# Self attention of the first layer: from pairs of tiles, phase by phase, to four tiles staggered in one step

## What is computed

```
xn = layernorm(x)                                   # over 256 values
q, k, v = xn @ in_proj.T + in_proj_bias             # 16 heads of 16
s = q @ k.T / 4 + alibi_slope[head] * (j - i)       # row i, column j, causal
p = maximum(softmax(s), 1e-10)
x = x + (p @ v) @ out_w.T + out_b
```

## Time and profile before

| | us |
|---|---|
| median of three runs | 8161.44 |
| the profiled execution: its time | 8200.94 |
| the profiled execution: its span | 8199.2 |
| TensorE matmul busy in the span | 6635.7 (81%) |
| VectorE busy | 5436.6 (66%) |
| ScalarE busy | 4031.7 (49%) |
| GpSimd busy | 2661.4 (32%) |

### The profile page before, as it was taken

How to read it: one execution, slowest core, us unless ns; L and a number is a source line. 1 busy time by engine, 2 the same in 40 slices (tenths; PEclk the granted TensorE clock), 3 DMA queues, 4 the chain that set the end, 5 groups by cost and what they waited for, 6 DMA issues and landing times. The chain is left out here.

```text
span 8199.2 us, 201722 instructions
## 1 busy us (share of the span) xinstructions
PE 6635.7 (81%) x71072; PEld 4742.2 (58%) x71073; DVE 5436.6 (66%) x11534; ACT 4031.7 (49%) x7817; POOL 2661.4 (32%) x4595
## 2 busy tenths in 40 slices
PE   5666999987727888888888888888888888799484
PEld 4556899964414555555555555555555555588442
DVE  5556666654237777777777777777778877544464
ACT  1112333321216666666666666666666666355121
POOL 0000000012124455454554554554555555200402
PEclk7777888888958888888988898988889988688597
DMA  0000000011210000000000000000000000000212
GB/s 28 0 0 15 5 4 4 4 43 55 88 42 12 14 11 13 13 11 13 13 11 13 11 13 13 13 11 13 11 13 13 13 11 14 8 10 8 95 61 92
DMA packets 136074, 172.62 MB, mean 21 GB/s; under 512 B 29104, under 2 KB 110096, under 8 KB 135184
## 3 DMA queue, kind: packets, MB, share of 16 engines
q1 hardware_dynamic: 122896, 135.34, 5.4%
q0 software_dynamic: 13056, 35.67, 1.4%
HBM read 128.74 MB, written 42.21 MB: 21 GB/s over the span
## 5 line engine op out<-in xcount | busy, mean ns | idle before, releaser
L1365 POOL MEMSET m_earlier<- 128x64 f32 x2 | 0.3, 152 | 2233.1 <-POOLq L2850 2233.1
L2693 PEld LDWEIGHTS d_ps_tx<-d_W,d_NT 64*64 64x64 f32 x10240 | 384.8, 145 | 398.8 <-issue 398.7
L2615 PE MATMUL d_ps_kv<-d_xnT,d_wqkv 128*128 (+1 forms) x1024 | 594.6, 710 | 4.2 <-DVE d_y L2235 3.2
L2235 DVE SCALAR_TENSOR_TENSOR d_y<-d_ps_kv,d_head,d_y 128x504 f32<-128x504 f32 (+2 forms) x768 | 556.3, 724 | 62.8 <-ACT d_y L2456 44.0
L2275 DVE TENSOR_TENSOR d_kq<-d_qkv,d_pre 128x512 f32<-128x512 f32 x768 | 530.4, 691 | 96.1 <-issue 92.9
L2321 DVE TENSOR_TENSOR d_W<-d_W,d_ps_tx 128x256 f32<-128x256 f32 x512 | 214.2, 418 | 458.3 <-PE d_ps_tx L2705 458.3
L2693 PE MATMUL d_ps_tx<-d_W,d_NT 64*64 64x64 f32 x10240 | 473.0, 236 | 49.6 <-DVE d_W L2321 39.9
L2680 PEld LDWEIGHTS d_ps_level<-d_kq,d_ks 128*64 128x64 f32 x10240 | 420.9, 166 | 150.3 <-DVE d_kq L2275 101.4
L2680 PE MATMUL d_ps_level<-d_kq,d_ks 128*64 128x64 f32 x10240 | 496.9, 257 | 3.3 <-DVE d_kq L2275 3.3
L2153 POOL TENSOR_TENSOR d_lnu<-d_lnu,d_z 128x512 f32<-128x512 f32 x128 | 163.1, 1275 | 1019.9 <-ACT d_lnu L2497 1019.9
L2119 POOL TENSOR_TENSOR d_roots<-d_radicand,d_power 128x20 f32<-128x20 f32 x128 | 459.8, 3592 | 10.0
(11 more groups left out here) (462 smaller groups left out, 17846.9 us busy)
## 6 DMA issues: line engine op xcount, KB each, us to landing
d_wqkv<-in_d_wqkv SPq DMA_DIRECT2D x128, 384.0 KB, 3.1
m_xg<-m_rows_in SPq DMA_DIRECT2D x144, 128.0 KB, 2.0
m_rows_out<-m_ye SPq DMA_DIRECT2D x144, 128.0 KB, 1.7
b_ctx<-in_ctx SPq DMA_DIRECT2D x64, 128.0 KB, 2.0
d_wg<-in_d_wg SPq DMA_DIRECT2D x128, 64.0 KB, 2.7
x_sb<-in_x SPq DMA_DIRECT2D x8, 512.0 KB, 7.5
m_wgu<-in_m_wgu SPq DMA_DIRECT2D x2, 2048.0 KB
out<-x_sb SPq DMA_DIRECT2D x8, 512.0 KB, 5.7
```

The source lines that it names most:

```text
L2235: ins = nc.vector.scalar_tensor_tensor(out3, in3, head[A.i][:, tap:tap + 1], out3, ALU.mult, ALU.add)
L2615: last = nc.tensor.matmul(ps_qkv[j], wqkv[u.i][:, j, kt, :], xnT[:, kt, tokens(u)], start=(kt == 0), stop=(kt == KT - 1))
L2693: last = nc.tensor.matmul(ps_t[rows, j * S:(j + 1) * S], NT[rows, l - 1, j, :], W[i][rows, 0, j, :], start=True, stop=True)
```

## The change

`l0_attention` is rewritten in the manner of the cross attentions. Each step works on four tiles in four stages. PSUM is divided by use instead of by tile: four banks for scores (`ps_s`), two for turned probabilities (`ps_p`), one for the front (`ps_f`: rows, query and key projection, queries, keys) and one for the back (`ps_b`: values, attended sums, output projection). Queries and keys go into one padded tile, in which each of the two sequences has its own 16 of 32 columns, with zeros in the rest; so a head's scores of both sequences come from one product (16 in place of 32 per tile), and the keys are turned by a product with `fold`. Attend has weights and data exchanged: its weights are the values, what streams are the probabilities, and its sums come out turned, in four groups of 32 partitions; the transposes and copies of the attended sums are left out. The keys' copy goes to ScalarE, the add of the output bias to GpSimd.

```diff
+        fold = mem.sbuf("a0_fold", [P, S])
-        bank = mem.banks("a0")
+        ps_s = mem.psum("a0_ps_s", [P, PER, 512])
+        ps_p = [mem.psum(f"a0_ps_p{i}", [P, 512])[:, :] for i in range(2)]
+        ps_f, ps_b = (mem.psum(f"a0_ps_{n}", [P, 512])[:, :] for n in ("f", "b"))
...
+                def bias_rows(u):
+                    hold(sems["xn_ready"], u.n)
+                    nc.gpsimd.tensor_tensor(x_sb[:, u.t, :], x_sb[:, u.t, :], bo[:, :], ALU.add).then_inc(sems["biased_x"], 1)
...
+                first(nc.vector.tensor_tensor(fold[:, :], ident[:, 0:S], ident[:, S:P], ALU.add))
...
+                def pads(u):
+                    dve.wait_ge(sems["qk_ps"], u.n)
+                    wait_positive(dve, sems["k_ps"], u.n - 2)
+                    for b in range(SEQS):
+                        rows = slice(b * S, (b + 1) * S)
+                        last = nc.vector.tensor_tensor(qkpad[u.i][rows, :, :, b * DH:(b + 1) * DH], ps_f[rows, :].rearrange("p (j h d) -> p j h d", j=2, h=H),
+                                                       bqkv[rows, 0:2, :].rearrange("p j (h d) -> p j h d", h=H), ALU.add)
+                    last.then_inc(sems["pads_ready"], 1)
...
+                def probs_out(u, part):
+                    dve.wait_ge(sems[f"p{part}_ps"], u.n)
+                    wait_positive(dve, sems["attended_ps"], u.n - 2)
+                    nc.vector.tensor_scalar(pT[u.i][:, 4 * part:4 * part + 4, :], ps_p[part].rearrange("p (c n) -> p c n", c=4), 1e-10, None,
+                                            ALU.max).then_inc(sems[f"p{part}_ready"], 1)
...
+                def vector_step(A, B, C, D):
+                    if A:
+                        normal(A)
+                    if D:
+                        probs_out(D, 0)
+                    if C:
+                        divide(C)
+                        values_out(C)
+                    if D:
+                        probs_out(D, 1)
+                    if B:
+                        bias_scores(B)
+                    if A:
+                        pads(A)
+                    if B:
+                        shift(B)
+                    if D:
+                        add_out(D)
+
+                tile_steps(dve, vector_step, TILES, 4)
...
+                def scalar_step(A, B, C, D):
+                    if C:
+                        exponents(C)
+                    if B:
+                        keys_out(B)
+                    if A:
+                        tokens_out(A)
+                    if D:
+                        attended_out(D)
+                    if A:
+                        queries_out(A)
...
+                def turn_keys(u):
+                    pe.wait_ge(sems["qT_ready"], u.n)
+                    for c in range(QUADS):
+                        h = c * PER
+                        last = nc.tensor.matmul(ps_f[:, c * S:(c + 1) * S], qkpad[u.i][:, 1, h:h + PER, :].rearrange("p h d -> p (h d)"), fold[:, :], start=True, stop=True)
+                    last.then_inc(sems["k_ps"], 1)
...
+                def values(u):
+                    pe.wait_ge(sems["xnT_ready"], u.n)
+                    wait_positive(pe, sems["v_ready"], u.n - 1)
+                    wait_positive(pe, sems["added"], u.n - 2)
...
+                def scores(u):
+                    hold(sems["kT_ready"], u.n)
+                    hold(sems["biased"], u.n - 1)
+                    for h in range(H):
+                        c, slot = divmod(h, PER)
+                        r = slot * SLOT
+                        last = nc.tensor.matmul(ps_s[:, slot, c * S:(c + 1) * S], qT[u.i][r:r + SLOT, c, :], kT[u.i][r:r + SLOT, c, :], start=True, stop=True)
+                    last.then_inc(sems["scores_ps"], 1)
...
+                def attend(u):
+                    pe.wait_ge(sems["p0_ready"], u.n)
+                    pe.wait_ge(sems["p1_ready"], u.n)
+                    pe.wait_ge(sems["v_ready"], at_most(u.n + 1, TILES))
+                    wait_positive(pe, sems["added"], u.n - 1)
+                    for k in range(KT):
+                        for b in range(SEQS):
+                            for r in range(PER):
+                                c = k * PER + r
+                                at = k * P + b * S
+                                last = nc.tensor.matmul(ps_b[r * SLOT:(r + 1) * SLOT, at:at + S], vblk[u.i][:, b, c, :, :].rearrange("p j d -> p (j d)"),
+                                                        pT[u.i][:, c, b * S:(b + 1) * S], start=True, stop=True, tile_position=(0, r * SLOT))
+                    last.then_inc(sems["attended_ps"], 1)
...
+                def tensor_step(A, B, C, D):
+                    if B:
+                        turn_keys(B)
+                    if C:
+                        values(C)
+                    if A:
+                        turn_rows(A)
+                    if B:
+                        scores(B)
+                    if A:
+                        project_pairs(A)
+                    if C:
+                        turn_probs(C, 0)
+                        turn_probs(C, 1)
+                    if D:
+                        attend(D)
+                    if A:
+                        turn_queries(A)
+                    if D:
+                        out_projection(D)
```

More of the change, by code:

```diff
@@ new lines, in attended_out @@
+                def attended_out(u):
+                    act.wait_ge(sems["attended_ps"], u.n)
+                    wait_positive(act, sems["y_ps"], u.n - 2)
+                    nc.scalar.copy(oT[u.i][:, :, :], ps_b[:, 0:D].rearrange("p (k n) -> p k n", k=KT)).then_inc(sems["oT_ready"], 1)
+                def scalar_step(A, B, C, D):
[9 more added lines that the diff above has]
+                        queries_out(A)
@@ new lines, in _, with hold, turn_rows, project_pairs @@
+                pe.wait_ge(sems["cleared"], 1)
+                def hold(sem, value):
+                    if not isinstance(value, int) or value > 0:
+                        pe.wait_ge(sem, value)
+                        pe.sem_inc(sems["held"], 1)
+                def turn_rows(u):
+                    pe.wait_ge(sems["xn_ready"], u.n)
+                    wait_positive(pe, sems["kT_ready"], u.n - 1)
+                    transpose_tile(nc, ps_f, xn[u.i], ident).then_inc(sems["xT_ps"], 1)
+                def project_pairs(u):
+                    pe.wait_ge(sems["xnT_ready"], u.n)
+                    for j, wt in enumerate((wq, wk)):
+                        for k in range(KT):
+                            last = nc.tensor.matmul(ps_f[:, j * D:(j + 1) * D], xnT[u.i][:, k, S:S + P], wt[:, k, :], start=(k == 0), stop=(k == KT - 1))
+                    last.then_inc(sems["qk_ps"], 1)
@@ new lines, in values @@
+                def values(u):
+                    pe.wait_ge(sems["xnT_ready"], u.n)
+                    wait_positive(pe, sems["v_ready"], u.n - 1)
+                    wait_positive(pe, sems["added"], u.n - 2)
+                    for b in range(SEQS):
+                        for k in range(KT):
+                            last = nc.tensor.matmul(ps_b[:, b * D:(b + 1) * D], xnT[u.i][:, k, b * P:(b + 1) * P], wv[:, k, :], start=(k == 0), stop=(k == KT - 1))
+                    last.then_inc(sems["v_ps"], 1)
@@ new lines, in out_projection @@
+                def out_projection(u):
+                    pe.wait_ge(sems["oT_ready"], u.n)
+                    for k in range(KT):
+                        last = nc.tensor.matmul(ps_b[:, 0:D], oT[u.i][:, k, :], wo[:, k, :], start=(k == 0), stop=(k == KT - 1))
+                    last.then_inc(sems["y_ps"], 1)
+                def tensor_step(A, B, C, D):
[14 more added lines that the diff above has]
+                        attend(D)
+                    if A:
+                        turn_queries(A)
+                    if D:
+                        out_projection(D)
```

207 lines of the change are left out of this document (88 added, 119 removed).

## The result

The changed kernel takes 7882.81 us (median of five executions, 7870.59 to 7899.23), the kernel before 8170.16 (median of five, 8159.08 to 8182.43): a ratio of 0.9655, 95% interval 0.9636 to 0.9675. The forecast was 7889, range 7855 to 7960. The profiled execution is the median one, with a span of 7881.1 us. The two traces are 318.1 us apart, 31 more than the medians, because the kernel before was profiled in a long execution.

The account below looks back on a forecast made before the run. The old stage was bound by a chain across engines, the new step by VectorE: 29 x 11.3 + 50 + 4 = 382 us in place of 654.6, 272.6 less than 8161.4, so 7889 us; range 7855 to 7960.

Parts of the forecast that it names:

- Rivals 1, 4 and 5: New stage: TensorE bound by clock, 7931, chance 0.15; slower than before, 8211, 0.03; no stagger, 8161, 0.02.
- rival 5: New stage: a wait in each step prevents the stagger, one tile's chain of about 20 us remains; 8161, chance 0.02.
- the signs of being wrong: Profile after: VectorE under 85% busy with waits for ps_s, ps_p or y_ps, clock near 0.7, or issue gaps every pass.
- VectorE's sum: VectorE's operations in one full step of the new stage, start to start, add up to 10.93 us.
- allowance for handovers and clock: Full step taken as 11.3 us, between 10.93 (VectorE alone) and 11.9 (clock 0.80), for handovers between nearly equal engines.
- TensorE's sum: TensorE's work in one full step at full clock: 9.49 us, or 8.64 to 10.73 with attend at its ends.
- Rival 2: Attend's weight loads do not overlap its matmuls, so TensorE's work bounds the step at 12.3 us; 7922, chance 0.12.
- The clock: TensorE's granted clock in the new stage: 0.85 to 0.9 expected; at 0.87 its 9.49 us become 10.9.
- The ring: Handovers through single banks ps_f and ps_b in a step: every term has slack, the exponents least with 0.3 us.
- Filling, draining, pause: Six partial steps at the stage's ends, 50 us (at most 66), plus one TensorE stall entering the loop, 4 us.
- Rival 3: The stall at the loop returns in each of 13 passes: 12 more of 4 us, 7937, chance 0.04.
- Nothing after the barrier changes: The phases behind the first self attention keep their times; only that stage gains, 272.6 us.

Follow-up runs that it names:

- e5: The changed kernel with the copy of the turned keys back on VectorE; 7896.9 us, 11.27 us a step.
- e6: The changed kernel with the multiplication by the reciprocal on GpSimd instead of VectorE; 7847.39 us, ratio to the kernel before 0.9604.
- e1: The changed kernel with attend in its old orientation, its copy and transposes back, still staggered; 7890.6 us, ratio to the kernel before 0.9655.
- e3: The changed kernel with the eight matmuls of the query and key projection issued twice; 7954.5 us, 11.39 us a step.
- e7: The changed kernel without the padding that aligns the loops of its three staggered phases; 7865.5 us.
- e11: The kernel before without the padding in front of the loops of its two cross attentions; 8159.8 us, ratio 0.9967.
- e12: The changed kernel with the reciprocal's multiplication on GpSimd and no padding ahead of staggered loops or the second layer's self attention loop; 7813.28 us, ratio 0.9544.

## Why the prediction was right, and where its sizes were off

**The mechanism held.** VectorE's work sets the step (e5, e6), TensorE and the handovers are cover. Rivals 1, 4 and 5 did not come about: the clock in the loop is 1.00, also at 95% TensorE load in e1, and a step is 10.93 us long, not the 20 of rival 5. Of the signs that were named, the length of the phase, VectorE above 90% and the vanished waits came; the step (11.3 us), TensorE's share (near 95%, measured 83% of a step), attend (57 ns, measured 20) and the clock (0.85 to 0.9, measured 0.98) did not. None of the signs of being wrong showed.

**VectorE's sum, 10.93 us, was met to 0.01.** Single terms moved by up to 0.12 (start to start: subtraction 1.26 for 1.14, biased scores 1.34 for 1.44, values 1.02, pads 1.41). The forecast of 11.3 failed in its allowance for handovers and clock, 0.37 us a step or 11 us in all: in an order in which everything VectorE needs is ready, handovers cost it nothing.

**TensorE's sum** was 9.49 and is 9.06 by its groups (9.05 as the 10.93 less the waits of 0.62 and 1.26, and 9.05 busy). Attend was mis-sized most: 1.82 taken, bounds 0.97 to 3.06, and 0.65 measured, below both. All other groups but the output projection came out 0.07 to 0.22 longer than scaled, together 0.74 (keys 1.08 against 0.86, values 1.81, projection 1.83, probabilities 0.97), which gave back most of attend's 1.17. Neither moved the step.

**Rival 2** did not come about. All 32 instructions of attend use all 128 rows, and 20 ns each is below what 64 streamed columns would take alone, 54 ns by the 216 for 256. The loads lie beside them, in the same step's timeline of the weight loads:

```profile
206.97 1.59 PEld L367 LDWEIGHTS a_ps_b<-a_wv,a_xnT 128*128 128x128 f32 x8 [0.72 <-issue]
...
212.96 0.49 PEld L397 LDWEIGHTS a_ps_b<-a_pT,a_vblk 128*32 128x32 f32 x32 [0.17 <-issue]
```

So loads and matmuls of different column groups ran side by side, against the rule of the Trainium skill that the prediction weighed (TensorE: Matmul & The Clock Gate, Part 3). The first of the two rows speaks against it as well: the values' eight loads, of all rows and all columns, take 1.59 us within the 1.81 of their eight matmuls. The earlier trace rows had shown as much before the result, with 11.15 us of loads beside 12.00 of matmuls in 12.00 us, so the chance of 0.12 leaned on a rule that the rows already doubted. Another page of the Trainium skill (TensorEngine Tiling (Array Packing), Key Properties) says that different tiles can load weights and multiply in parallel, and the trace agrees, 20 ns against 58 in e1's two groups of 64 columns.

**The clock** was taken as 0.87 from the other staggered phases; it was 1.00, so how much a lower one would have cost was not seen. TensorE had 1.9 us to spare.

**The ring** was drawn with slacks of 1.9 us at the pads. e3 measured 1.27.

**Filling, draining, pause.** 378.0 less 29 steps of 10.93 and 4.4 for the pause leaves 56.6 us, where 50 was taken. The pause was sized at 4 us on TensorE; it came on ScalarE, with 5.78, of which 4.4 showed. Rival 3, a pause in each pass, is out: one in 13.

**"Nothing after the barrier changes"** was wrong by some 13 us: the padding in cross 0 (e7, e11).

**The sum:** 378 for 382, minus 13 from padding, and a median of before that was 9 us higher with five executions than with three. The errors nearly cancel, and so that the forecast came within 6 us is in part luck; a forecast with right sizes from the same base, 8161.4 - 276.5 - 12.7 = 7872, would have come out 11 us too low where the one given was 6 too high.

## What to carry to other kernels

Add up each engine's start-to-start times in a staggered step: the largest sum was the step here, since each operand was ready, and the next bound was the longest ring through a shared buffer, which doubling one operation on it measured (9.66 us). What an edit is worth depends on the order it stands in: 115 us where all is one chain, 12 us under cover. Compare phases that did not change before crediting a total: padding ahead of loops moved one by 13 us, and a phase of 4800 us differed by 24 us along with its clock.

## What the runs showed of the hardware that was not expected

- 32 matmuls of 32 weight columns in four column groups, 64 columns streamed, take 0.65 us, or 20 ns each; the same products in two groups of 64 weight columns, 32 streamed, take 1.85 us, 58 ns each.
- With padding ahead of a loop one engine or another issues nothing for 5.6 to 15.0 us once; without it there is no such pause at that loop, in the first pass or later (e7, e12), and two to five packets of the instruction queues are fewer.
- GpSimd multiplies 128x1024 values in 1.90 us beside a VectorE 98% busy; the VectorE operations beside it here, which read PSUM, keep their lengths.
- TensorE with two waits a step of 0.6 and 1.3 us keeps a granted 1.00 from 115 to 395 us. After it stood still for 3.6 us in the first looped step, the granted clock was 0.50 from 111.3 to 114.6 us, and four matmuls of 256 columns took 1.93 us in place of 1.13.
